# Last layernorm's row sums on ScalarE's accumulator, and the softmax tiles normalised by GpSimd instead of VectorE

## The reference, cut to what matters

```python
x = L0_attn_x                                              # (8, 512, 128)
h = layernorm(x) * (1 + ca) + sa
x = x + ga * (layernorm(linear_attention(h)) * gamma + beta)
h = layernorm(x) * (1 + cb) + sb
# the feed-forward part, in which this change lies
h = h + msa(layernorm(h) * ln1_w + ln1_b)                  # 16 heads of 8, softmax over 512 keys
h = h + moe(layernorm(h) * ln2_w + ln2_b)                  # 8 experts, the best one per token
x = x + gb * h

def msa(x):
    attn = softmax(q @ k.T / sqrt(8))                      # exp(s) / sum(exp(s))
    return (attn @ v) @ w_proj
```

## Time and profile before

| | before |
|---|---|
| median of 3 runs | 689.78 us (689.75 to 690.06) |
| the profiled execution | 690.73 us |
| its span, first to last instruction | 688.9 us |
| mean granted TensorE clock | 0.971 of full speed |
| PE busy in the span | 615.9 us (89%) |
| DVE busy | 586.3 us (85%) |
| ACT busy | 503.4 us (73%) |
| POOL busy | 414.9 us (60%) |

### The profile page before, as it was taken

The page is one execution under the profiler, slowest core; times in us unless marked ns, Lnnn a source line. Parts: engine busy times, 40 slices in busy tenths (PEclk is TensorE's granted clock), DMA queues, the critical chain, the costliest instruction groups (busy, mean ns, idle before and its releaser), DMA issues.

```text
span 688.9 us, 16395 instructions
## 1 busy us (share of the span) xinstructions
PE 615.9 (89%) x5313; PEld 308.2 (45%) x5313; DVE 586.3 (85%) x1481; ACT 503.4 (73%) x1079; POOL 414.9 (60%) x931
## 2 busy tenths in 40 slices
PE   4688789988877898899999999999999999899994
PEld 3355556665544222223233232332323322589993
DVE  6886999998877988899999999999999994776552
ACT  3653777788655378888888888888888889755661
POOL 4411567667655743436676887887877862566553
PEclk9998999999999589999999999999999999999998
DMA  6564143335354121137120301203012010456510
GB/s 182 154 236 131 38 131 125 121 126 184 115 162 139 47 92 47 47 97 240 35 61 2 116 25 48 81 13 116 24 41 89 13 47 22 141 172 182 159 34 9
DMA packets 42899, 66.25 MB, mean 96 GB/s; under 512 B 7948, under 2 KB 36335, under 8 KB 39808
## 3 DMA queue, kind: packets, MB, share of 16 engines
q1 hardware_dynamic: 39232, 56.73, 27.8%
q0 software_dynamic: 3296, 8.41, 3.4%
q10 hardware_dynamic: 288, 0.07, 0.0%
HBM read 41.64 MB, written 22.26 MB: 93 GB/s over the span
## 4 chain that ended last, share of the span: by engine, by line
PE 53%; ACT 20%; DVE 11%; issue 6%; SPq 5%; POOL 3%; DMA 2%; ACTq 0%; POOLq 0%; DVEq 0%
PE bank L1118 12%; ACT arena L2082 10%; PE pair L1107 8%; PE bank L1079 7%; PE pair L1366 4%; DVE arena L1619 3%; DVE arena L1437 2%; PE bank L1129 2%; PE pair L1375 2%; PE bank L1375 2%; ACT arena L2051 2%; PE pair L1159 2%; PE bank L960 1%; PE pair L1079 1%; POOL arena L683 1%
## 5 line engine op out<-in xcount | busy, mean ns | idle before, releaser
L2082 ACT ACTIVATE arena<-pair 128x512 f32<-128x512 f32 x506 | 278.1, 603 | 52.6 <-PE pair L1107 50.6
L1619 DVE TENSOR_REDUCE arena<-bank 128x1 f32<-128x512 f32 x388 | 251.4, 682 | 10.1 <-PE bank L1079 7.1
L1107 PE MATMUL pair<-q_stack,k_stack 64*128 64x512 bf16 x506 | 158.1, 386 | 5.9 <-ACT arena L2082 5.1
L1079 PE MATMUL bank<-k_stack,q_stack 63*128 63x512 bf16 x388 | 136.6, 396 | 8.9 <-DVE arena L1619 4.8
L1118 PE MATMUL bank<-arena,values 128*9 128x512 f32 x1024 | 134.5, 597 | 1.6 <-ACT arena L2082 1.5
L1437 DVE TENSOR_TENSOR arena<-bank,cst 128x512 f32<-128x512 f32 x128 | 82.0, 682 | 16.5 <-PE bank L946 16.1
L1619 DVE TENSOR_REDUCE arena<-pair 128x1 f32<-128x512 f32 x124 | 84.3, 680 | 2.4 <-PE pair L1079 2.0
L748 POOL TENSOR_TENSOR arena<-arena 128x32 f32<-128x32 f32 (+6 forms) x312 | 68.4, 219 | 24.4
L1079 PEld LDWEIGHTS bank<-k_stack,q_stack 63*128 63x128 bf16 x388 | 33.1, 93 | 110.1 <-ACT arena L2087 24.8
L1107 PEld LDWEIGHTS pair<-q_stack,k_stack 64*128 64x128 bf16 x506 | 40.6, 93 | 47.4 <-ACT arena L2082 21.4
L1079 PE MATMUL pair<-k_stack,q_stack 63*128 63x512 bf16 x124 | 49.0, 395 | 0.5 <-ACT arena L2103 0.3
(11 more groups left out here) (318 smaller groups left out, 1222.1 us busy)
## 6 DMA issues: line engine op xcount, KB each, us to landing
softmax_parts<-arena SPq DMA_DIRECT2D x8, 768.0 KB, 4.1
q_stack<-softmax_parts SPq DMA_DIRECT2D x48, 128.0 KB
k_stack<-softmax_parts SPq DMA_DIRECT2D x48, 128.0 KB
linear_parts<-arena SPq DMA_DIRECT2D x7, 768.0 KB, 3.7
q_stack<-linear_parts SPq DMA_DIRECT2D x42, 128.0 KB
k_stack<-linear_parts SPq DMA_DIRECT2D x42, 128.0 KB
arena<-in_L_ffn_w_dram SPq DMA_DIRECT2D x16, 256.0 KB, 4.4
v_all<-token_rows SPq DMA_DIRECT2D x20, 192.5 KB, 2.8
```

Source lines behind the costliest of these rows:

```text
L1079: pe.matmul(bank[:], qs[b % 2][rows, slot, qt * P:(qt + 1) * P], ks[b % 2][rows, slot, :], start=True, stop=True).then_inc(d_s_m, 1)
L1107: pe.matmul(score_bank(s)[:], ks[u][rows, 2 * g + x, kt * P:(kt + 1) * P], qs[u][rows, 2 * g + x, :], start=True, stop=True).then_inc(d_s_ ...
L1619: dve.reduce_max(mx[:, m % 2, col:col + 1], bank[:], AX).then_inc(d_s_mr, 1)
L2082: act.activation(pt[:, kt % 2, x, half, :], score_bank(s)[:], ACT.Exp, scale=SCALE).then_inc(d_s_e, 1)
```

## The change

For steps 4 to 29 (tiles f = 0 to 25) the division leaves VectorE. At the beginning of pass 2 ScalarE copies the 16 x 9 used columns of the turned bank into SBUF (`d_turned_out`, 128 x 144), which also frees the bank. GpSimd then raises the 16 denominators to the power -1 (128 x 16) and multiplies (`d_normalise` in its loop, ahead of `rows_of`). The last tiles keep VectorE's path.

For the 24 rows of `rows_of` the sums are taken by ScalarE: `row_sum` (a copy of y with the accumulator, after the second exponential of pass 0) and `row_squares` (Square of row sum - 128 y, with the accumulator, after the fourth exponential of pass 0). GpSimd keeps the two small scalings, the power, one scaling with two operands, and `row_rest`.

The core of the diff:

```diff
@@ GpSimd
-                def total(src):
-                    w = D // 2
-                    while w:
-                        done(pool.tensor_tensor(half[:, 0:w], src[:, 0:w], src[:, w:2 * w], ALU.add))
-                        after()
-                        src, w = half, w // 2
+                def d_normalise(f):
+                    pool.wait_ge(d_s_fr, f + 1)
+                    done(pool.tensor_tensor(d_den[:, f % C, :], nine[:, :, E], minus_one[:], ALU.pow))
+                    after()
+                    pool.tensor_tensor(d_on[:, f % C, :].rearrange("p (h e) -> p h e", h=H), nine[:, :, 0:E],
+                                       d_den[:, f % C, :].unsqueeze(2).to_broadcast([P, H, E]), ALU.mult).then_inc(d_s_fo, 1)
...
-                    pool.wait_ge(d_s_fh, f + 1)
                     wait(pool, d_s_xn, f)
                     wait(pool, d_s_xy, f)
-                    total(y)
-                    done(pool.tensor_scalar(nm[:], half[:, 0:1], -1.0 / D, None, ALU.mult))
-                    after()
-                    done(pool.tensor_scalar(cen[:], y, nm[:], None, ALU.add))
-                    after()
-                    done(pool.tensor_tensor(sq[:], cen[:], cen[:], ALU.mult))
-                    after()
-                    total(sq)
-                    done(pool.tensor_scalar(ve[:], half[:, 0:1], 1.0 / D, LN_EPS, ALU.mult, ALU.add))
+                    pool.wait_ge(d_s_su, f + 1)
+                    done(pool.tensor_scalar(nm[:], row_su[:, u:u + 1], -1.0 / D, None, ALU.mult))
+                    pool.wait_ge(d_s_sq, f + 1)
+                    done(pool.tensor_scalar(ve[:], row_sq[:, u:u + 1], 1.0 / D ** 3, LN_EPS, ALU.mult, ALU.add))
...
-                    pool.tensor_scalar(row_slot(f)[:, 0:D], cen[:], rs[:], None, ALU.mult).then_inc(d_s_xn, 1)
+                    pool.tensor_scalar(row_slot(f)[:, 0:D], y, nm[:], rs[:], ALU.add, ALU.mult).then_inc(d_s_xn, 1)
...
                 for n in range(G, NB):
+                    if n < NB - 2:
+                        d_normalise(n - G)
                     if G < n <= LAST + G:
                         rows_of(n - G - 1)
@@ TensorE, maximum: the fourth maximum matmul of pass 2
-                        pe.wait_ge(d_s_fo, n - G + 1)
+                        pe.wait_ge(d_s_fr, n - G + 1)
@@ VectorE
-                                if j == 0 and kt == 2 and n >= G:
-                                    d_normalise(n - G, ring_bank(n, 1, 4))
...
-                        if kt == 1 and n >= G:
+                        if kt == 1 and n + 2 >= NB:
                             d_denominators(n - G, ring_bank(n, kt, 4))
-                            if n + 2 >= NB:
-                                d_normalise(n - G, ring_bank(n, kt, 4))
+                            d_normalise(n - G, ring_bank(n, kt, 4))
@@ ScalarE
+                def row_sum(f):
+                    act.wait_ge(d_s_fh, f + 1)
+                    wait(act, d_s_su, f)
+                    wait(act, d_s_xn, f - 1)
+                    act.activation(seen[:, 0], h[:, f, 0:D], ACT.Copy, accum_out=row_su[:, f % 2:f % 2 + 1]
+                                   ).then_inc(d_s_su, 1)
+                def row_squares(f):
+                    act.wait_ge(d_s_su, f + 1)
+                    wait(act, d_s_sq, f)
+                    act.activation(seen[:, 1], h[:, f, 0:D], ACT.Square, bias=row_su[:, f % 2:f % 2 + 1], scale=-float(D),
+                                   accum_out=row_sq[:, f % 2:f % 2 + 1]).then_inc(d_s_sq, 1)
+                def d_turned_out(f, bank):
+                    act.wait_ge(d_s_ft, f + 1)
+                    wait(act, d_s_fo, f)
+                    act.activation(nine[:], bank[:].rearrange("p (h w) -> p h w", h=H)[:, :, 0:E + 1], ACT.Copy
+                                   ).then_inc(d_s_fr, 1)
...
                         for i in range(4):
+                            if i == 0 and kt == 2 and G <= n < NB - 2:
+                                d_turned_out(n - G, ring_bank(n, 1, 4))
                             probs(n, kt, i)
+                            if i == 1 and kt == 0 and G < n <= LAST + G:
+                                row_sum(n - G - 1)
                             if i == 2 and kt == 0 and n:
                                 d_numerators_out(n - 1)
+                            if i == 3 and kt == 0 and G < n <= LAST + G:
+                                row_squares(n - G - 1)
```

More of the change, by code:

```diff
@@ L321, in program @@
         gatew, shift = d([NE]), d([P])
-        half, cen, sq, gy = d([D]), d([D]), d([D]), d([D])
+        seen, gy = d([2, D]), d([D])
+        row_su, row_sq = d([2]), d([2])
+        nine, minus_one = d([H, E + 1]), d([H])
         nm, ve, rs = d([1]), d([1]), d([1])
@@ L359, in program @@
         s_y, s_yc = sem_early("b_projected"), sem_early("b_projected_out")
-        c_s_st = [sem_early(f"c_stats{m}") for m in range(3)]
-        c_s_mv = [sem_early(f"c_means{m}") for m in range(3)]
+        c_s_st = [None] + [sem_early(f"c_stats{m}") for m in range(1, 3)]
+        c_s_mv = [None] + [sem_early(f"c_means{m}") for m in range(1, 3)]
         c_s_ve = [sem_early(f"c_variances{m}") for m in range(3)]
         c_s_rs = [sem_early(f"c_rstd{m}") for m in range(3)]
-        c_s_nm = [sem_early(f"c_mean_turned{m}") for m in range(3)]
-        c_s_nb = [sem_early(f"c_shift{m}") for m in range(3)]
+        c_s_nm = [None] + [sem_early(f"c_mean_turned{m}") for m in range(1, 3)]
+        c_s_nb = [None] + [sem_early(f"c_shift{m}") for m in range(1, 3)]
         c_s_n = [sem_early(f"c_normed{m}") for m in range(3)]
@@ L412, in program @@
         d_s_pl, d_s_xn, d_s_xy = sem("d_pool_step"), sem("d_last_normed"), sem("d_rows_ready")
+        d_s_su, d_s_sq = sem("d_row_sums"), sem("d_row_squares")
         d_s_st, d_s_mv, d_s_ve = sem("d_end_stats"), sem("d_end_means"), sem("d_end_variances")
@@ L788, in rows_of @@
                 def rows_of(f):
-                    y = h[:, f, 0:D]
-                    pool.wait_ge(d_s_fh, f + 1)
+                    y, u = h[:, f, 0:D], f % 2
                     wait(pool, d_s_xn, f)
                     wait(pool, d_s_xy, f)
-                    total(y)
-                    done(pool.tensor_scalar(nm[:], half[:, 0:1], -1.0 / D, None, ALU.mult))
-                    after()
-                    done(pool.tensor_scalar(cen[:], y, nm[:], None, ALU.add))
-                    after()
-                    done(pool.tensor_tensor(sq[:], cen[:], cen[:], ALU.mult))
-                    after()
-                    total(sq)
-                    done(pool.tensor_scalar(ve[:], half[:, 0:1], 1.0 / D, LN_EPS, ALU.mult, ALU.add))
+                    pool.wait_ge(d_s_su, f + 1)
+                    done(pool.tensor_scalar(nm[:], row_su[:, u:u + 1], -1.0 / D, None, ALU.mult))
+                    pool.wait_ge(d_s_sq, f + 1)
+                    done(pool.tensor_scalar(ve[:], row_sq[:, u:u + 1], 1.0 / D ** 3, LN_EPS, ALU.mult, ALU.add))
                     after()
@@ L869, in _ @@
                 done(pool.memset(rows_low[:, 0], 0.0))
+                done(pool.memset(minus_one[:], -1.0))
                 after()
```

## The result

| | before | after |
|---|---|---|
| median | 689.76 us (4 runs, 688.19 to 690.06) | 767.44 us (4 runs, 765.58 to 770.92) |
| ratio to before | | 1.113, 95% interval 1.109 to 1.117 |
| the profiled execution | 690.73 us | 768.29 us |
| its span | 688.9 us | 766.5 us |
| mean granted TensorE clock | 0.971 | 0.934 |

The change costs 77.7 us. The forecast was 742.5 with a range from 721 to 758: the sign and the place were right, the size was short by 25 us.

A forecast was written before the change was run, and what follows sets the result against it. TensorE, with two stalls of 0.31, was taken to set the 10.59 us step. Adding 0.29, 1.95 and 0.12 less 0.31 gave 12.64; over the steps 52.7 us on 689.78, so 742.5, range 721 to 758.

The forecast's parts named there:

- The sum: Whole kernel at full clock: 24 steps at +2.05 and two at +1.76, 52.7 us in total, giving 742.5.
- The bound and the two stalls: Softmax step of 10.59 us: TensorE's own work 9.97, plus stalls of 0.31 in pass 1 and 0.31 in pass 3.
- The relief of VectorE: Reciprocal 0.34 and product 0.20, together 0.54 us a step, leave VectorE's queue in steps 4 to 29.
- No more than the pass 3 stall of 0.31 can come back: TensorE at 9.97 is late next, so VectorE's relief returns 8 us at the very best.
- The sums on ScalarE: Pass 0: `row_sum` delays the fourth exponential and pass 1's third score matmul by 0.29; `row_squares` costs nothing.
- I take nothing: `row_squares`, after pass 0's fourth exponential, moves the next exponentials by 0.29, but they are 0.4 or more ahead of need.
- The division on GpSimd: Before `d_turn_back`: the power over 128 x 16 takes 2.91 us, stalling TensorE 1.95 us in every step.
- I treat that extra as unchanged: The extra time of the six steps that also carry the choice of experts stays as it was.
- The clock falls as well: Rival, chance 0.08: a tenth of the softmax stage at half clock, TensorE's work growing some 26 us, about 760.
- a small part of the clock: The range's upper end, 758, also takes in a little of a clock fall.
- partly inside the stalls: In the clock rival, some of TensorE's 26 us growth would be hidden in its waiting time.

The follow-up runs named there:

- w1: The change with row sums later in ScalarE's queue, VectorE taking reciprocals from ScalarE's copy in pass 2, GpSimd only the product: 688.54 us, 0.998 of before.
- w2: As w1, but VectorE takes the reciprocals from the turned bank at the end of pass 1 and ScalarE copies after it: 686.51 us, 0.995 of before.
- e1: From the changed kernel, the division goes back to VectorE and the row sums stay on ScalarE: 697.81 us, 1.012 of before.
- e4: The changed kernel plus eight matmuls of 512 columns in steps 4 to 29, before TensorE's wait for the turning back: 742.33 us, 1.078 of before.
- e5: The changed kernel with the power over only 8 of the 16 denominators, the other 8 copied: 714.31 us, 1.035 of before.

## Why the prediction was wrong

The sum at full clock held. What failed is the step behind it, the fall of the clock, to which the forecast gave a small chance and which it kept almost wholly out of its range.

- *The bound and the two stalls.* Right. The step was coupled as described, and its marks came out within 0.2 us.
- *The relief of VectorE.* "No more than the pass 3 stall of 0.31 can come back" held, but it counted reciprocal and product alike. w1 and w2 show that the reciprocal was hidden by `d_turn`: with it at its old place an ordinary step gains 0.19, so of the 0.54 only the product's 0.20 was worth something.
- *The sums on ScalarE.* The 0.29 of `row_sum` was exact (2.64 and 3.31). "I take nothing" for `row_squares` was wrong: I looked only at the exponentials behind it, and not at `maxima_out`, which stands there too and empties the bank of the fourth maximum matmul of pass 1 (462.43, released by L2084). With bias and scale it also takes 0.38 (460.79 to 461.17). That matmul comes at 4.76 of the step instead of 4.33 (425.24 in the trace of before), of which 0.29 is `row_sum` and 0.14 `row_squares`. e1 puts both sums together at 8 us.
- *The division on GpSimd.* Right: 2.91 forecast, 2.94 measured, stall 1.95 forecast and 1.93 measured. By the rule of the Trainium skill ("GPSIMD Engine Reference", section 3.1, Elementwise) reciprocal and product would have cost 1.06 us, an estimate from that page; the trace doesn't agree for a power, which alone takes 2.94. For the product of 128 x 128 it comes nearer: 0.41 against VectorE's 0.28, 1.5 times.
- *The sum.* 52.7 forecast at full clock; e4, in which the clock doesn't fall, measures 53. That it is this close is partly luck. In step 16 the turning back came 0.20 later than forecast and what follows it was 0.07 shorter, so an ordinary step is 0.13 too long (12.77). "I treat that extra as unchanged" erred the other way: a step with the choice of experts was 0.6 to 0.75 longer than an ordinary one before and is 0.4 longer in after at full clock (13.14 to 13.18).
- *The clock.* This is the step that failed. "The clock falls as well" stood among the rivals with 0.08 and about 760, while the range up to 758 took in "a small part of the clock". It was argued from two stretches of the earlier trace rows, one that kept the clock and one that didn't, and the new step lay between them: that gives no reason for so small a chance. The price was low too: 25 us came, not 18. The 26 us by which TensorE's work was to grow was a good size; what failed is "partly inside the stalls". Between the two stretches shown above TensorE's busy time grows by 1.50 (10.28 to 11.78) and the step by 1.46, so next to nothing is hidden; in the stretch shown the low clock lies in pass 3, behind the standstill.

What the runs show of the cause: after has a standstill of 1.9 us in each step and loses the clock in over half of them; e4 has steps of the same length, with the standstill filled, and holds it; e5, standing for 0.82 us, holds it too. So it is TensorE's lack of work there that brings the clock down. They don't settle where between 0.82 and 1.9 us the fall begins. Nor do they part the length of the one standstill from how little TensorE has to do in the step as a whole, because filling or shortening the standstill changes both. Both stay open.

## What to carry to other kernels

A step moved to another engine is priced by that engine's rows for that very operation, at two sizes: where they differ, take the slope to the new size before anything else. A new wait on TensorE costs its length and may cost the clock as well; where some stretch of the trace of before lost the clock while TensorE waited for others, that case deserves real weight and a price of its own. What is taken off a full engine is worth only what stood between its work when others weren't waited for, and the same few small instructions can cost 8 us in all or nothing by their place in the queue.

## What the runs showed of the hardware

- GpSimd's power costs 0.57, 1.04, 1.67 and 2.94 us for 1, 4, 8 and 16 elements on 128 partitions, about 0.157 for each (the first two with the exponent -0.5, the others with -1); a product of 128 x 16 costs 0.22.
- With a standstill of TensorE of 1.93 us in each step of 12.8 the clock fell to its lower level in 13 of 23 steps, 1.46 us for each, 25 us in the whole kernel. Eight matmuls of no use in that standstill brought the 25 us back.
- ScalarE's Square of 128 x 128 with a bias operand and the accumulator takes 0.38 us of its queue, the copy with the accumulator 0.30.
